# A gated cross-attention and expert kernel: forty matmuls on ones at the start, and four moves in the order of work

## What is computed

```python
# x, ctx_1024: (16, 256, 256)
def xattn(q, c, wq, wk, wv):
    Q = c @ wq;  K = q @ wk;  V = q @ wv
    return softmax(Q @ K.T, axis=2) @ V
def ffn(x, Wg, W1, W2, W3):                     # E=8, D=256, H=704, top 2
    scores = xt @ Wg.T
    topk_scores, topk_idx = top_k(scores, 2)
    y = (silu(xt @ W1[e].T) * (xt @ W2[e].T)) @ W3[e].T      # for every expert e
    return sum over the two chosen experts of score * y
x = x + tanh(g_xattn) * xattn(ctx_1024, layernorm(x), wq, wk, wv)
x = x + tanh(g_ffn)   * ffn(layernorm(x), Wg, W1, W2, W3)
```

## Time and profile before

| | us |
|---|---|
| median of 3 runs | 609.45 |
| lowest, highest | 607.35, 613.29 |
| the profiled execution, time | 606.95 |
| its span, first to last instruction | 605.1 |
| TensorE busy in it | 573.3 |
| VectorE, ScalarE, GpSimd busy | 323.4, 329.6, 261.5 |
| mean granted TensorE clock | 0.993 |

### The profile page before, as it was taken

One profiled execution on the slowest core, in us unless ns is written; L12 is line 12 of the kernel. 1 busy time (PEld: TensorE's weight loads), 2 busy tenths in 40 slices (PEclk: granted clock), 3 DMA queues, 4 the chain that ended last, 5 costly groups with the idle time before them and its releaser, 6 DMA issues.

```text
span 605.1 us, 14783 instructions
## 1 busy us (share of the span) xinstructions
PE 573.3 (95%) x4765; PEld 503.7 (83%) x4765; DVE 323.4 (53%) x861; ACT 329.6 (54%) x473; POOL 261.5 (43%) x244
## 2 busy tenths in 40 slices
PE   5999999999889999979999999999999999999994
PEld 4777888788778999969999889889989889888783
DVE  2588887978687777754334334334334334333322
ACT  3887988798665455425435445445445445344441
POOL 4056474637157887642432432432432432433323
PEclk9999999999899999989999999999999999999999
DMA  7667688767513343452223223223233223223322
GB/s 233 198 197 235 205 262 259 210 193 221 169 40 126 93 83 75 108 134 46 40 51 56 41 45 64 39 48 60 38 48 61 40 47 63 38 38 46 57 33 26
DMA packets 52371, 61.50 MB, mean 102 GB/s; under 512 B 7632, under 2 KB 46160, under 8 KB 52304
## 3 DMA queue, kind: packets, MB, share of 16 engines
q1 hardware_dynamic: 34656, 38.15, 21.2%
q0 software_dynamic: 13296, 18.23, 17.7%
q10 hardware_dynamic: 4352, 4.20, 2.0%
HBM read 36.90 MB, written 23.66 MB: 100 GB/s over the span
## 4 chain that ended last, share of the span: by engine, by line
PE 74%; DVE 10%; DMA 4%; issue 4%; ACT 4%; POOL 3%; SPq 0%; POOLq 0%; ACTq 0%; DVEq 0%
PE psum L929 34%; PE psum L958 21%; PE psum L804 8%; PE psum L938 4%; DMA w_in<-in_W3T 3%; PE psum L858 2%; DVE w_lo L1069 2%; PE psum L842 1%; PE psum L797 1%; POOL rows_by_expert L567 1%; DVE nmax L1128 1%; DVE xa L1140 1%; ACT w_hi L677 1%; DVE w_lo L1062 1%; PE psum L947 1%
## 5 line engine op out<-in xcount | busy, mean ns | idle before, releaser
L599 POOL DMA_INDIRECT out<-w_in,id_s x71 | 129.1, 1818 | 232.2 <-ACT w_in L752 134.3
L929 PE MATMUL psum<-arena,w_hi 128*128 128x256 f16 x1408 | 211.2, 273 | 1.5 <-DVE xa L1140 1.2
L929 PEld LDWEIGHTS psum<-arena,w_hi 128*128 x1408 | 137.0, 98 | 17.9 <-issue 2.0
L929 PE MATMUL psum<-arena,w_lo 128*128 128x256 f16 x704 | 134.4, 273 | 0.0
L567 POOL DMA_INDIRECT rows_by_expert<-xn2r,slot_i x64 | 75.8, 1184 | 29.1 <-issue 19.3
L684 ACT ACTIVATE arena<-psum 128x1024 f16<-128x1024 f16 (+1 forms) x39 | 36.9, 946 | 92.6 <-PE psum L858 92.6
L1352 DVE SCALAR_TENSOR_TENSOR arena<-psum,h_unit,arena 128x1280 f32<-128x1280 f32 x32 | 49.6, 1550 | 66.1 <-PE psum L929 66.1
L929 PEld LDWEIGHTS psum<-arena,w_lo 128*128 x704 | 68.9, 98 | 8.0
L804 PE MATMUL psum<-arena 128*128 128x256 f32 x256 | 64.3, 396 | 1.1 <-ACT arena L634 0.5
L728 ACT ACTIVATE arena<-psum,w_unscale 64x256 f32<-64x256 f32 x32 | 15.0, 467 | 90.4 <-PE psum L929 90.4
L958 PE MATMUL psum<-w_hi,w_in 128*128 x385 | 54.5, 276 | 3.8 <-ACT w_in L752 3.8
(11 more groups left out here) (182 smaller groups left out, 880.3 us busy)
## 6 DMA issues: line engine op xcount, KB each, us to landing
xa<-rows_by_expert SPq DMA_DIRECT2D x71, 136.0 KB, 2.2
w_in<-in_W1T SPq DMA_DIRECT2D x8, 704.0 KB, 4.8
w_in<-in_W3T SPq DMA_DIRECT2D x8, 640.0 KB, 5.4
w_in<-in_W2T SPq DMA_DIRECT2D x8, 640.0 KB, 4.9
arena<-in_ctxT SPq DMA_DIRECT2D x16, 256.0 KB, 6.4
xa<-in_x SPq DMA_DIRECT2D x16, 256.0 KB, 6.0
out<-xa ACTq DMA_DIRECT2D x16, 256.0 KB, 5.5
out<-w_in,id_s POOLq DMA_INDIRECT x71, 4.3
```

The source lines that it names most:

```text
L599: pool.indirect_dma_start(out=out[:, :], out_offset=bass.IndirectOffsetOnAxis(ap=id_s[:, t8:t8 + 1], axis=0), in_=y_s[:, t8 % 4, :], in_of ...
L929: ins = pe.matmul(flat_ps[:, j * N2:(j + 1) * N2], w12[w_part][:, c, bass.ds(e * (2 * H) + j * P, P)], xg_t[:, k, x_part, c, :], start=(q ...
```

## The change

Line numbers in the words below are those of the kernel before; the diff has them on its left.

1. PE begins with a wait for POOL's first memory fill and forty matmuls of the constant `ones` (128x128, bf16) by itself, into bank 7, which nothing reads before it is written again. POOL fills `ones` ahead of `ident` for that.
2. DVE waited at its very beginning for all of POOL's constants (`s_const`); now it waits for them behind `centre()`.
3. The plan of the first eight pairs is made at the end of step 14 and not of step 13.
4. In slot 6 POOL issued the scatter of the last batch and then the add for the second tile of pair 4; now the add comes first.
5. `to_output` waited for `s_lo` ahead of its first matmul. Now it waits for `s_hi`, does the ten matmuls that need the high part alone, waits for `s_lo`, and does the other seven. It is the same 17 matmuls.

```diff
+    WARM = 40
@@ gpsimd
+            pool.memset(ones[:], 1.0).then_inc(s_pool, 1)
             pool.memset(ident[:], 0.0).then_inc(s_pool, 1)
-            pool.memset(ones[:], 1.0).then_inc(s_pool, 1)
...
@@ gpsimd, expert loop
-                if i == len(AT_PAIR):
-                    scatter(B - 1)
...
                 if i >= 2 and pair(i - 2):
                     add_rows(i - 2, 1)
-                if i in range(1, len(AT_PAIR)):
+                if i - 1 in AT_PAIR:
                     scatter(AT_PAIR[i - 1])
@@ tensor
+            pe.wait_ge(s_pool, 1)
+            for _ in range(WARM):
+                pe.matmul(bank[7][:, 0:P], ones[:], ones[:], start=True, stop=True)
             pe.wait_ge(s_wk, 16)
             pe.wait_ge(s_centred, 3)
@@ tensor, to_output
-                pe.wait_ge(s_lo, i + 1)
+                pe.wait_ge(s_hi, i + 1)
                 at_least(pe, s_y_copied, t)
-                parts = [(c, 0, c) for c in range(KH)] + [(c, 1, c) for c in range(KH)] + [(KH + c, 0, c) for c in range(KF)]
+                parts = [(c, w_part, c) for w_part in range(2) for c in range(KF)]
+                parts += [(KF, 0, KF), (KF, 1, KF)] + [(KH + c, 0, c) for c in range(KF)]
                 for q, (c, w_part, r) in enumerate(parts):
+                    if q == 2 * KF:
+                        pe.wait_ge(s_lo, i + 1)
@@ vector
-            dve.wait_ge(s_const, CONSTS)
...
             centre()
+            dve.wait_ge(s_const, CONSTS)
...
-                if n == COUNT_STEP:
+                if n == COUNT_STEP + 1:
                     full_pairs()
```

## The result

The changed kernel takes 605.41 us (median of 20 runs, 602.60 to 608.60), the kernel before 608.76 us (20 runs beside it, 604.24 to 613.29). The ratio is 0.9948, with a 95% interval of 0.9928 to 0.9967: about 3.3 us less, real but within 1%. The forecast was 602.1 us, a gain of 6.3. So about half of the gain did not come. Medians and ratios here leave out single executions in the chip's slower state (one of `changed_again`, one of `const_only`, and a few of the kernel before beside them). The profiled execution took 605.58 us (span 603.6) against 606.95 (span 605.1), 1.4 us less.

The account below looks back on a forecast made before the run. PE was taken as the bound, at full rate from slot 1 on, so gains lay only at three places: 0.8 + 4.4 + 1.1 = 6.3 us off 608.4 gives 602.1 us, range 599 to 607.

Parts of the forecast that it names:

- The start: First 20 us: PE some 3 us sooner, but W2's landing caps what is kept at 0.8 us gain.
- the second rival: Start: PE waits near 1.8 us for W1's squares, the clock falls, -1.0 instead of +0.8; 603.9 us, chance 0.12.
- the rival of the late gather: Steps 14 to 15: gather comes later, a 2.6 us wait and half clock eat the 4.5; 605.9 us, chance 0.19.
- The plan: Steps 13 to 15: stall of 2.6 us and half clock go, new gather wait of 1.2 us; gain 4.4 us.
- The last tile: Last output tile: PE starts on the high part without waiting for the low part; gain 1.1 us.
- the wait inside the group: `to_output`, 71 tiles: a second wait, possibly 2.0 us in all, taken as 0.
- the order of the high parts in the other 70 tiles: `to_output` before the last tile: the low part was ready already, so reordering gains nothing, 0.
- the add ahead of the scatter: Slot 6 on POOL: gain and loss 0, and the stall of 3.8 us with its half clock stays.
- The rival of an exposed weight load: `to_output`: the new wait exposes a weight load of 99 ns per tile, 7.0 us; 609.1 us, chance 0.05.

Follow-up runs that it names:

- changed_again: The changed kernel run once more, unchanged, on another occasion beside the kernel before: 605.08 us, ratio 0.9973.
- const_only: The kernel before with only DVE's wait for the constants moved behind the centring: 608.60 us, ratio 1.0027.
- warm_only: The kernel before with only the forty matmuls at PE's beginning and the fill of `ones` first: 609.77 us, ratio 1.0042.
- fill: The changed kernel with 44 more matmuls on `ones` ahead of the first sum of squares: 601.92 us, ratio 0.9922.
- fill_again: The changed kernel with 44 more matmuls on `ones` ahead of the first sum of squares, run once more: 603.09 us, ratio 0.9942.
- no_warm: The changed kernel without its forty matmuls at PE's beginning: 604.70 us, ratio 0.9959.
- slot7_only: The kernel before with only 60 matmuls on `ones` in slot 7, ahead of the output that PE waits for: 606.08 us, ratio 0.9976.
- before_again: The kernel before run once more, unchanged: 606.50 us, ratio 1.0000.
- plan_only: The kernel before with only the plan of the first eight pairs moved from step 13 to step 14: 604.24 us, ratio 0.9949.
- output_only: The kernel before with only the new order in `to_output`, high parts first and the low-part wait mid-group: 606.76 us, ratio 0.9979.
- fill_scatter_first: The changed kernel with 44 more matmuls on `ones` ahead of the first sum of squares and slot 6's scatter before the add again: 604.60 us, ratio 0.9927.

## Why the prediction was wrong, and where it was right

**The start is the step that failed.** The forecast gave it +0.8 us, with the reason that DMAs cap PE's 3 us lead at the landing of W2, and put PE's wait in front of that cap at nothing. It was right that a DMA is the cap, but the one that comes first is W1, and the wait for it has a price. The time that PE would need to reach the first sum was worked out, 12.6 against squares ready at 14.3, but in the second rival, at 0.12, and the forecast itself let PE pass it free. The wait was forecast there at 1.8 us and measured at 2.53 (3.10 in the second execution), the clock fell, and the start came out at -1.5 us by the second sum and -1.8 by step 14; that rival said -1.0. By its time, 603.9, it was nearer to 605.4 than the forecast was. Nearer still, at 605.9, was the rival of the late gather, but by luck: its mechanism did not happen, since the gather's wait was 1.28 us and the clock stayed at 1.00 behind it. `warm_only` shows the effect without the rest, 1.0042; `fill` and `fill_again` show the scores back at full speed once the gap is full. That the gap opens without the forty (`no_warm`) says that the moved constant wait alone is close to it; by itself (`const_only`) it did not open it, with W1's squares 0.66 us earlier and PE 1.26 us later than there.

The case against the rival was the stall of 2.2 us at 1.00 in the last tile. That was one example, and in two other executions with the same stall, 2.15 us long (`slot7_only`, `warm_only`), the clock did fall behind it. The rule quoted there, from the Trainium skill, TensorE: Matmul & The Clock Gate, "Loop structure matters more than you think", speaks of a long wait for a DMA ahead of every group of matmuls, behind which they run cold; here it is a single wait, for ACT's squares of what the DMA brought. The outcome agrees in all four executions in which PE waited 1.9 us or more for W1's squares: the matmuls behind ran at half clock. It does not for each wait of that length, as `before_again`, `const_only` and `fill_again` show.

Even the +0.8 was wrong in kind. It came from one execution, in which W2 had landed 0.8 us before its squares. Over 17 executions W1's squares began at 12.94 to 14.20 us, and this scatter is larger than the term. What it forecast can be seen once: with the gap full and W1 early (`fill`), W2's squares began at 19.80, for 19.7 forecast and 20.52 before. In the changed kernel they began at 22.02.

**The plan** was right in mechanism and a little large: 4.4 forecast, 3.6 in the profiled executions. The stall and the half clock went; the wait for the gather was 1.28 us against 1.2 forecast, the clock stayed 1.00 behind it, and the residual's stall went. What was missing: PE waits 0.9 instead of 0.5 us for the turned probabilities, and between the sum of squares and the scores of step 15 0.35 us more pass (they start at 161.99 and 162.48; before, at 164.40 and 164.54). The plan's own weight in the median is 3.1 us (`plan_only`).

**The last tile** was right at the group: 1.1 forecast, 1.2 measured. The forecast stopped there and took PE's gain as the program's. Behind it stand ACT's copy and the last add, and that add waits for the DMA of the add before it, which had not moved as far: -0.8 us. This term was missing. `output_only` shows the same wait, 2.48 us.

**At nothing**: the wait inside the group, the order of the high parts in the other 70 tiles, and the add ahead of the scatter were costed at 0. Groups of 17 at 1.86 us and the stall of 3.8 us with either order (`fill`, `fill_scatter_first`) agree. The rival of an exposed weight load (609.1) is refuted. The gap of 0.68 us in slot 2 was in no other execution, and its cause stays open.

The sum of the terms as measured in the two profiled executions is 1.5; by the medians 3.3. The difference lies in which executions were profiled: that of the kernel before is 1.8 us below its median, that of the changed one 0.2 above, and the kernel before ranges over 9 us in 20 runs. The parts' own ratios (plan -3.1, `to_output` -1.3, forty +2.6, constants +1.6 us) add up to -0.2 us where the whole gives -3.3; each is uncertain by 1.5 to 2.5 us, so this is no proof that the parts act on each other. Why executions of one kernel differ by a fall of the clock at 124, 266 or 594 us remains open. The fall near 124 us came in three executions (`no_warm`, `warm_only`, `changed_again`), all of them among the four with the gap at the start; whether the late start brings it on was not tested.

## What to carry to other kernels

Before adding a warm-up, or anything that brings PE to work earlier, find the first operand that PE can't have sooner and work out how long PE then stands there: a lead that ends in front of a DMA is turned into a gap, and the gap can cost more than the lead. Work put into that gap kept the clock through the matmuls behind it in all seven executions here; work put ahead of it did not in any of three. But a lead that is carried past one gap ends in the next, so look at that one too. And follow a gain at the last matmul to the last write: the write may wait for the one before it.

## What the runs showed of the hardware

- The granted clock reads 1.00 over the first matmuls, but they run at half speed: eight of 128x256 f32 took 3.75 us there without the forty and 1.96 to 2.57 with them, and the forty took 4.07 us where 44 of the same later took 2.62.
- A stall of 3.8 us left the clock at 1.00 in two executions (`before_again`, `const_only`); in another the clock fell behind one of 1.43 us (`no_warm`).
- One issue of the x load on SP's queue took 2.61 us at 6.36, where its neighbours took 0.4 to 0.8; the same issue took 0.47 us in the kernel before and 2.15 in `before_again`, so this is scatter between executions and not the change.
- An indirect add to `out` with another ahead of it waited 2.4 to 2.9 us for that one's DMA, in all eleven executions that had the new order in `to_output`.
